# Householder steps of a tridiagonalization: fewer operations on GpSimd, a longer vector chain in another order

## The chip, the cores and the metric

One Trainium2 chip, one of its cores. The time is the device time in microseconds (us) of one execution of the whole program. A core has five engines with a queue each: PE (TensorE, matrix products), DVE (VectorE), ACT (ScalarE), POOL (GpSimd) and SP (SyncE, which issues the transfers here). Each engine works through its queue in order, and the engines meet only at semaphores.

## The reference, cut to what matters

A graph layer over a batch of 128 matrices `x[b]` of 120 nodes by 1024 features. One 120x120 adjacency matrix serves the whole batch:

```
degv = A.sum(0) + A.sum(1) - diagonal(A);  dinv = degv ** -0.5
Ln = dinv[:, None] * (diag(degv) - A) * dinv[None, :]
_, U = eigh(Ln)                                  # 120x120, once
h = relu(layernorm(x))                           # every b
agg = einsum('vn,bvd->bnd', U, h)
x1 = relu(agg @ W1 + b1) @ W2 + b2
... a non-local attention block over the 1024 positions (512 pooled keys) gives w_y ...
z = w_y + x1
out = x + einsum('nv,bvd->bnd', U, z) + z
```

The change is wholly inside `eigh`, in the reduction of `Ln` to tridiagonal form. That reduction is 118 Householder steps. With `v` the row of the remaining matrix below the pivot and `L = 120 - k` columns left in step `k`, a step makes the reflector `u = v + sign(v1)|v| e1`, scales it by `2/(u.u)`, and takes two rank-one products off the matrix, the second factor of which is `w = A u * scale + (a multiple) * u`.

## The kernel before, in words

The program has two phases. The first ends when the eigenvectors and everything folded into them are ready; until then it also does, for each batch element, the part of the layer norm and of the product with `W1` that doesn't need `U`. The second phase, 2685 us long, runs the attention block of every batch element and is not touched by the change.

In the first phase two chains run side by side:

- The eigenvectors, mostly on DVE. 118 Householder steps (`reflect`), then a grid count of eigenvalues, two finer sweeps, the vectors of the tridiagonal matrix, and their back-transformation. Of the latter, the product of all reflectors (`factor`) is made by PE, ACT and POOL beside DVE's work.
- The batch work ("pieces"), mostly on ACT. For batch element `t`, ACT makes relu and the sum of squares, PE transposes the result (4 pieces of 2 transposes, L684), ACT copies it out of PSUM (`fT`), PE multiplies it with `W1` (8 pieces of one product, L694), and ACT copies the result. That is 12 pieces for a batch element. ACT starts each with the relu of L533.

PE has one queue for both. Its order is written out by hand: in each Householder step it takes first the product for the row (L714), then some of the step's 9 pieces, then the two products of the rank-two update (L720, L721), then the rest of the pieces. The constant `LN_RATE` sets the 9, `LN_BEHIND` how many of them come after the update (2, so 7 come before it). After the last step the queue holds the remaining pieces, and among them `factor(i)` before batch element `WY_SLOT + 1 + i`, and the grid count's product (L791), which waits for DVE's grid, before batch element `GRID_AT` (98). Three small products that fold the vectors in (L772, L776, L780) stand after batch elements 127, 128 and 129.

One Householder step on DVE and its partners, by line:

- PE: L714 makes two rows, `A u`-like (partition 0 of `ps_V`) and the pivot row (partition 32).
- DVE: L1006 copies the pivot row to `row1`; L1008 adds `DU = sign * root` to `u[1]`; L1010 makes `z` from both rows and `DU`; L1012 makes `u.u`; L1014 the dot product of `u` and `z` (into `AC`); L1017 the reciprocal; L1020 times the gate (-1, or 0 for a null vector); L1022 `AC` times that; L1023 the scaled reflector `cu`; L1025 the second factor in place of `z`, which releases PE (`w_ready`).
- PE: L720, L721, the rank-two update into `ps_up`, which releases `up_ready`.
- DVE: L1029 and L1031 make the next `u` out of the row, `cu` and the second factor; L992 and L994 its squared norm without and with the first element (`XN`, `S2`); L1036 the next pivot column into `XI`; L1040 adds the update to `QA` in place, which releases the next step's L714 (`a_ready`); L1041 keeps a column.
- POOL (`shift`): L447 and L448 the sign, after `u_ready`; L450 the square root by `pow`, after `S2`; L451 `DU`, which L1008 waits for; L452 the gate. In steps 1 to 8 `fill` adds some memsets behind that.

In the code `need(i)` is a wait for DVE's own earlier instruction, `did` counts it, `T`, `TS` and `STT` are `tensor_tensor`, `tensor_scalar` and `scalar_tensor_tensor`.

## Time and profile before

| | |
|---|---|
| median of 3 runs | 3352.58 us (3351.86 to 3355.92) |
| the profiled execution: its own time | 3354.83 us |
| the profiled execution: span of the trace | 3353.1 us |
| granted TensorE clock, mean over the span | 0.989 of full |
| PE busy | 3181.8 us (95%) |
| DVE busy | 2289.5 us (68%) |
| ACT busy | 2413.1 us (72%) |
| POOL busy | 1949.6 us (58%) |

The span is the time from the first to the last instruction of one profiled execution; its own time is 1.7 us longer. PE's share is an average over two phases that are limited in different ways. A matmul row's duration includes a modelled end, so rows of PE overlap, and a busy PE isn't PE at its peak.

### The profile page before, as it was taken

To read this page: it belongs to the slowest core of one execution; us is meant where nothing else is said; L and a number is where in the kernel's file an instruction comes from. 1 tells how busy PE (TensorE), PEld (TensorE's weight loads), DVE (VectorE), ACT (ScalarE), POOL (GpSimd) and SP (SyncE) were. 2 spreads that over 40 slices of the span, in tenths; PEclk is the share of its full clock that TensorE was granted. 3 is DMA by queue.
4 is the path that set the end of the run, shared out by engine and by line. 5 is a ranking of instruction groups with operands and counts; after the bars stand their busy time and mean duration, and the time that the engine had idled before them with its cause. 6 is when DMAs were issued, how large, how long until landed. Compare 5 with 4: busy or idle time off the path is not lost.

```text
span 3353.1 us, 65817 instructions
## 1 busy us (share of the span) xinstructions
PE 3181.8 (95%) x16040; PEld 2554.4 (76%) x16040; DVE 2289.5 (68%) x6009; ACT 2413.1 (72%) x4380; POOL 1949.6 (58%) x2073
## 2 busy tenths in 40 slices
PE   6888886799999999999999999999999999999997
PEld 5667776677777777777777777778777777777775
DVE  7777778866666666666666666666666666666664
ACT  6888998856666766666666667666666676666665
POOL 4333321146666666666666666666666666666665
PEclk9999999989999999999999999999999999999998
DMA  3333433312222222222222222222222222222222
GB/s 95 93 96 98 105 107 95 95 37 72 74 75 75 73 71 71 71 71 72 73 74 72 71 71 71 71 71 71 73 74 74 75 71 71 71 71 71 73 74 67
DMA packets 111576, 256.22 MB, mean 76 GB/s; under 512 B 47501, under 2 KB 49798, under 8 KB 111494
## 3 DMA queue, kind: packets, MB, share of 16 engines
q1 hardware_dynamic: 111493, 255.25, 27.8%
q8 instruction: 37, 0.61, 0.1%
q14 instruction: 46, 0.37, 0.0%
HBM read 190.69 MB, written 63.44 MB: 76 GB/s over the span
## 4 chain that ended last, share of the span: by engine, by line
PE 80%; DVE 10%; POOL 3%; issue 3%; ACT 3%; DVEq 0%; POOLq 0%; ACTq 0%
PE ps_M L800 8%; PE ps_M L801 8%; PE ps_M L802 8%; PE ps_S L877 7%; PE ps_E L800 7%; PE ps_O L800 7%; PE ps_E L801 7%; PE ps_O L802 7%; PE ps_E L802 7%; PE ps_O L801 7%; PE ps_M L861 3%; POOL sc L450 1%; ACT junkx L537 1%; DVE u L1031 1%; DVE rown L1029 1%
## 5 line engine op out<-in xcount | busy, mean ns | idle before, releaser
L503 POOL TENSOR_TENSOR p_lo<-p,p_hi 128x512 fp32r<-128x512 f32 x1024 | 1380.9, 1349 | 932.1 <-ACT p_hi L654 929.9
L649 ACT ACTIVATE p<-ps_E 128x512 f32<-128x512 f32 x1024 | 613.6, 599 | 332.6 <-PE ps_E L802 307.5
L1394 DVE TENSOR_REDUCE nmx<-ps_S 128x1 f32<-128x512 f32 x1024 | 658.8, 685 | 127.8 <-PE ps_S L877 124.7
L654 ACT ACTIVATE p_hi<-p 128x512 fp32r<-128x512 f32 x1024 | 647.2, 632 | 32.6
L800 PE MATMUL ps_E<-o_hi,Q_hi 123*128 123x512 f32 x1024 | 427.0, 417 | 0.0
L800 PE MATMUL ps_O<-p_hi,v_hi 128*121 128x512 f32 x1024 | 407.2, 398 | 4.2 <-POOL p_lo L503 4.2
L802 PE MATMUL ps_O<-p_lo,v_hi 128*121 128x512 f32 x1024 | 406.7, 397 | 0.0
L801 PE MATMUL ps_E<-o_hi,Q_lo 123*128 123x512 f32 x1024 | 404.4, 395 | 0.0
L801 PE MATMUL ps_O<-p_hi,v_lo 128*121 128x512 f32 x1024 | 404.4, 395 | 0.0
L802 PE MATMUL ps_E<-o_lo,Q_hi 123*128 123x512 f32 x1024 | 404.2, 395 | 0.0
L1374 DVE TENSOR_REDUCE gf<-ps_M 128x256 f32<-128x512 f32 x256 | 177.1, 692 | 261.8 <-PE ps_M L802 261.8
L877 PE MATMUL ps_S<-Q_hi,o_hi 122*128 122x512 f32 x1024 | 349.7, 402 | 2.2 <-DVE nmx L1394 1.1
L510 POOL TENSOR_TENSOR y<-y,acc 121x512 f32<-121x512 f32 x256 | 329.0, 1285 | 13.3 <-DVE y L1402 13.3
L800 PE MATMUL ps_M<-o_hi,Chi 122*128 122x512 f32 (+1 forms) x768 | 314.0, 409 | 2.3 <-DVE o_lo L1359 1.5
L802 PE MATMUL ps_M<-o_lo,Chi 122*128 122x512 f32 (+1 forms) x768 | 303.1, 395 | 0.0
L801 PE MATMUL ps_M<-o_hi,Clo 122*128 122x512 f32 (+1 forms) x768 | 303.0, 394 | 0.0
L694 PE MATMUL ps_m<-W1s,fT 128*120 128x128 f32 x2048 | 285.0, 285 | 7.1 <-ACT P L549 7.1
L1365 DVE TENSOR_REDUCE phf<-ps_M 128x256 f32<-128x512 f32 x256 | 175.7, 686 | 130.0 <-PE ps_M L802 130.0
L694 PEld LDWEIGHTS ps_m<-W1s,fT 128*120 128x120 f32 x2048 | 245.3, 187 | 24.6 <-issue 16.1
L877 PEld LDWEIGHTS ps_S<-Q_hi,o_hi 122*128 122x128 f32 x1024 | 194.0, 190 | 80.0 <-ACT mrow L639 26.5
L621 ACT ACTIVATE o_hi<-ps_M 120x512 fp32r<-120x512 f32 x256 | 153.2, 598 | 139.1 <-PE ps_M L802 139.1
L800 PEld LDWEIGHTS ps_E<-o_hi,Q_hi 123*128 123x128 f32 x1024 | 193.8, 189 | 49.5 <-issue 6.4
(363 smaller groups left out, 5947.7 us busy)
## 6 DMA issues: line engine op xcount, KB each, us to landing
rbc<-r_dram SPq DMA_DIRECT2D x128, 484.0 KB
xin<-in_x_dram SPq DMA_DIRECT2D x128, 480.0 KB, 4.2
xt<-in_x_dram SPq DMA_DIRECT2D x128, 480.0 KB, 4.9
out_dram<-y SPq DMA_DIRECT2D x128, 480.0 KB, 3.7
o_hi<-mrow SPq DMA_DIRECT2D x256, 2.0 KB
dcol<-y SPq DMA_DIRECT2D x128, 4.0 KB, 2.0
r_dram<-rcol SPq DMA_DIRECT2D x128, 4.0 KB, 1.4
W1s<-in_L_gnn_W_dram SPq DMA_DIRECT2D x1, 512.0 KB, 4.1
```

The costliest lines, as they stand in the source:

```text
L503: pool.tensor_tensor(p_lo[:, c % 4, :], p[:, c % 4, :], p_hi[:, c % 4, :].bitcast(F32), ALU.subtract).then_inc(plo_sb, 1)
L510: pool.tensor_tensor(y[:, par, f], y[:, par, f], acc[:, par, f], ALU.add).then_inc(y_sb, 1)
L649: act.activation(p[:, c % 4, :], ps_E[c % 2][:, :], ACT.Exp).then_inc(p_sb, 1)
L654: act.activation(p_hi[:, c % 4, :], p[:, c % 4, :], ACT.Copy).then_inc(phi_sb, 1)
L694: last = mm(ps_m[par][0:N, 0:H], fT[:, par, c * N:(c + 1) * N], W1s[:, c, :], start=(c == 0), stop=(c == KC - 1))
L800: mm(dst, whi, mhi, start=start, stop=False)
L801: mm(dst, wlo, mhi, start=False, stop=False)
L802: return mm(dst, whi, mlo, start=False, stop=stop)
L877: mm(ps_S[SBANK[c]][:, :], o_hi[0:NA, par, c * 128:(c + 1) * 128], Q_hi[0:NA, par, :], start=True, stop=True).then_inc(S_ps, 1)
L1365: dve.tensor_reduce(phf[:, j * 256:(j + 1) * 256], ps_M[BANK["ph" + piece[2]]][:, :].rearrange("p (m t) -> p m t", t=2), AX.X, ALU.max).th ...
L1374: dve.tensor_reduce(gf[:, j * 256:(j + 1) * 256], ps_M[BANK["g" + piece[2]]][:, :].rearrange("p (m t) -> p m t", t=2), AX.X, ALU.max).then ...
L1394: dve.tensor_reduce(nmx[:, c:c + 1], ps_S[SBANK[c]][:, :], AX.X, ALU.max, negate=True).then_inc(max_sb, 1)
```

## The change

In words: GpSimd keeps the root of `S2` and gets one new operation, `TWICE = u1 * REC * GATE2`, which goes back to DVE. Sign and gates are made by DVE (`sign`), behind the `QA` update of the step before. The root goes straight into `u[1]`, before the row is there. The row is copied with the sign multiplied in, ahead of `u.u`. `RG` is gone: `cu` is `u` times the reciprocal times a gate that holds the factor 2. The first half of the next reflector (`rown`, the part with `cu[1]`) is made before the second factor, and reads its row from PSUM. Its second half uses `PAIR`, the second factor's first element, made from `TWICE`, `AC` and `z`'s first element instead of being read from the second factor. `QA` is held twice, each step reads one copy and writes the other, and the wait of the update for `XI` is gone. One copy at the end brings the even columns together. One piece more comes after the update in each step (`LN_BEHIND` 3), the grid product moves behind one more batch element (`GRID_AT` 99), and `factor` begins two batch elements earlier (`WY_SLOT` 94).

```
@@ gpsimd, shift(k)
-                pool.wait_ge(u_ready, k + 1)
-                chain(pool.tensor_scalar(sc[:, SGN:SGN + 1], u[:, 1:2], 0.0, 2.0, ALU.is_ge, ALU.mult))
-                chain(pool.tensor_scalar(sc[:, SGN:SGN + 1], sc[:, SGN:SGN + 1], -1.0, None, ALU.add))
                 pool.wait_ge(s2_ready, k + 1)
-                chain(pool.tensor_tensor(sc[:, ROOT:ROOT + 1], sc[:, S2:S2 + 1], sc[:, 11:12], ALU.pow))
-                pool.tensor_tensor(sc[:, DU:DU + 1], sc[:, SGN:SGN + 1], sc[:, ROOT:ROOT + 1], ALU.mult).then_inc(du_ready, 1)
-                pool.tensor_scalar(sc[:, GATE:GATE + 1], sc[:, XN:XN + 1], TINY, -1.0, ALU.is_gt, ALU.mult).then_inc(gate_ready, 1)
+                pool.tensor_tensor(sc[:, ROOT:ROOT + 1], sc[:, S2:S2 + 1], sc[:, 11:12], ALU.pow).then_inc(root_ready, 1)
+                if k + 1 < STEPS:
+                    pool.wait_ge(rec_ready, k + 1)
+                    pool.tensor_scalar(sc[:, TWICE:TWICE + 1], u[:, 1:2], sc[:, REC:REC + 1], sc[:, GATE2:GATE2 + 1],
+                                       ALU.mult, ALU.mult).then_inc(twice_ready, 1)
@@ tensor, reflect
-                mm(ps_V[0:33, 0:L], XI[:, k + 1:k + 34], QA[:, k:N], start=True, stop=True).then_inc(ry_ready, 1)
+                mm(ps_V[0:33, 0:L], XI[:, k + 1:k + 34], QA[:, par * N + k:par * N + N], start=True, stop=True).then_inc(ry_ready, 1)
@@ vector
+            def sign():
+                i_ge = did(TS(s_(SGN), u[:, 1:2], 0.0, 2.0, ALU.is_ge, ALU.mult))
+                did(TS(s_(GATE), s_(XN), TINY, -2.0, ALU.is_gt, ALU.mult))
+                did(TS(s_(GATE2), s_(XN), TINY, -4.0, ALU.is_gt, ALU.mult))
+                need(i_ge)
+                TS(s_(SGN), s_(SGN), -1.0, None, ALU.add).then_inc(sign_ready, 1)
...
             def reflect(k):
+                dve.wait_ge(root_ready, k + 1)
+                dve.wait_ge(sign_ready, k + 1)
+                i_u = did(STT(out=u[:, 1:2], in0=s_(ROOT), scalar=s_(SGN), in1=u[:, 1:2], op0=ALU.mult, op1=ALU.add))
                 dve.wait_ge(ry_ready, k + 1)
-                i_row = did(dve.tensor_copy(row1[:, k:N], ps_V[32:33, 0:L]))
-                dve.wait_ge(du_ready, k + 1)
-                i_u = did(T(u[:, 1:2], s_(DU), u[:, 1:2], ALU.add))
-                need(i_row)
-                i_z = did(STT(out=z_(0), in0=row1[:, k:N], scalar=s_(DU), in1=ps_V[0:1, 0:L], op0=ALU.mult, op1=ALU.add))
+                i_row = did(TS(row1[:, k:N], ps_V[32:33, 0:L], s_(SGN), None, ALU.mult))
                 need(i_u)
                 i_uu = did(STT(out=srow[:, k:k + 1], in0=u[:, 1:2], scalar=u[:, 1:2], in1=s_(XN), op0=ALU.mult, op1=ALU.add))
+                need(i_row)
+                i_z = did(STT(out=zt[:, 0:L], in0=row1[:, k:N], scalar=s_(ROOT), in1=ps_V[0:1, 0:L], op0=ALU.mult, op1=ALU.add))
+                need(i_uu)
+                dve.reciprocal(s_(REC), srow[:, k:k + 1]).then_inc(rec_ready, 1)
                 need(i_z)
-                i_dot = did(STT(out=sqj[:, 0:L], in0=u[:, 0:L], scalar=1.0, in1=z_(0), ..., accum_out=s_(AC)))
-                need(i_uu)
-                i_rec = did(dve.reciprocal(s_(REC), srow[:, k:k + 1]))
-                dve.wait_ge(gate_ready, k + 1)
-                need(i_rec)
-                i_rg = did(T(s_(RG), s_(REC), s_(GATE), ALU.mult))
-                need(i_rg)
-                i_ac = did(T(s_(AC), s_(AC), s_(RG), ALU.mult))
-                i_cu = did(TS(cu[:, 0:L], u[:, 0:L], s_(RG), 2.0, ALU.mult, ALU.mult))
-                need(i_ac)
-                STT(out=z_(0), in0=u[:, 0:L], scalar=s_(AC), in1=z_(0), op0=ALU.mult, op1=ALU.add).then_inc(w_ready, 1)
+                i_dot = did(STT(out=sqj[:, 0:L], in0=u[:, 0:L], scalar=0.5, in1=zt[:, 0:L], ..., accum_out=s_(AC)))
+                dve.wait_ge(rec_ready, k + 1)
+                i_cu = did(TS(cu[:, 0:L], u[:, 0:L], s_(REC), s_(GATE), ALU.mult, ALU.mult))
+                need(i_cu)
                 if k + 1 < STEPS:
-                    need(i_cu)
-                    dve.wait_ge(w_ready, k + 1)
-                    need(did(STT(out=rown[:, k + 2:N], in0=z_(2), scalar=cu[:, 1:2], in1=row1[:, k + 2:N], ...)))
-                    STT(out=u[:, 1:L - 1], in0=cu[:, 2:L], scalar=zs[:, N + 1:N + 2], in1=rown[:, k + 2:N], ...).then_inc(u_ready, 1)
+                    i_part = did(STT(out=rown[:, 0:L - 2], in0=zt[:, 2:L], scalar=cu[:, 1:2], in1=ps_V[32:33, 2:L], ...))
+                need(i_dot)
+                STT(out=zs[:, N:N + L], in0=cu[:, 0:L], scalar=s_(AC), in1=zt[:, 0:L], op0=ALU.mult, op1=ALU.add).then_inc(w_ready, 1)
+                now, then = par * N, (1 - par) * N
+                if k + 1 < STEPS:
+                    dve.wait_ge(twice_ready, k + 1)
+                    i_pair = did(STT(out=s_(PAIR), in0=s_(TWICE), scalar=s_(AC), in1=zt[:, 1:2], op0=ALU.mult, op1=ALU.add))
+                    need(i_part)
+                    need(i_pair)
+                    STT(out=u[:, 1:L - 1], in0=cu[:, 2:L], scalar=s_(PAIR), in1=rown[:, 0:L - 2], ...).then_inc(u_ready, 1)
                     dve.wait_ge(u_ready, k + 2)
+                    dve.wait_ge(w_ready, k + 1)
                     norm(L - 1)
                     dve.wait_ge(up_ready, k + 1)
                     STT(out=XI[:, k + 2:k + 3], ...).then_inc(xcol_ready, 1)
-                    dve.wait_ge(xcol_ready, k + 2)
                 dve.wait_ge(up_ready, k + 1)
-                T(QA[:, k:N], QA[:, k:N], ps_up[0:N, 1:L + 1], ALU.add).then_inc(a_ready, 1)
+                dve.wait_ge(a_ready, k + 1)
+                T(QA[:, then + k:then + N], QA[:, now + k:now + N], ps_up[0:N, 1:L + 1], ALU.add).then_inc(a_ready, 1)
+                if k + 1 < STEPS:
+                    sign()
                 dve.tensor_copy(wyCT[0:N, k:k + 1], ps_up[0:N, 0:1]).then_inc(c_kept, 1)
...
+            need(did(dve.tensor_copy(QA[:, 0:STEPS:2], QA[:, N:N + STEPS:2])))
@@ constants
-LN_RATE, LN_LEAD, LN_BEHIND = (9, 1), 2, 2
-GRID_AT = 98
-WY_SLOT, WY_STEPS = 96, 19
+LN_RATE, LN_LEAD, LN_BEHIND = (9, 1), 2, 3
+GRID_AT = 99
+WY_SLOT, WY_STEPS = 94, 19
```

## Rows read from the trace of the kernel before

**Rows 1.** Windows: stretch, its length, each engine's busy time (instructions), PEclk, DMA.

```profile
360.00:468.00 108.00, 94.27 (x729) 79.90 (x727) 79.46 (x574) 100.66 (x184) 41.65 (x150) 1.00 0.40 104
668.00:3353.00 2685.00, 2658.36 (x12159) 2114.35 (x12158) 1761.23 (x2816) 1843.60 (x3328) 1736.16 (x1406) 0.99 0.26 71
```

**Rows 2.** Timeline of one step (L=75): start, duration, engine, line, out<-in.

```profile
200.63 0.15 DVE L1008 TENSOR_TENSOR u<-sc,u 1x1 f32<-1x1 f32 x1
...
201.03 0.20 DVE L1012 SCALAR_TENSOR_TENSOR srow<-u,sc 1x1 f32<-1x1 f32 x1
201.16 0.22 DVE L1014 SCALAR_TENSOR_TENSOR sqj<-u,zs 1x75 f32<-1x75 f32 x1
...
201.31 0.15 DVE L1017 RECIPROCAL sc<-srow 1x1 f32<-1x1 f32 x1
...
201.56 0.15 DVE L1020 TENSOR_TENSOR sc<-sc 1x1 f32<-1x1 f32 x1
...
201.82 0.24 DVE L1023 TENSOR_SCALAR cs<-u,sc 1x75 f32<-1x75 f32 x1
...
201.99 0.28 DVE L1025 SCALAR_TENSOR_TENSOR zs<-u,sc,zs 1x75 f32<-1x75 f32 x1
...
202.37 0.28 DVE L1029 SCALAR_TENSOR_TENSOR rown<-zs,cs,row 1x73 f32<-1x73 f32 x1
...
202.69 0.28 DVE L1031 SCALAR_TENSOR_TENSOR u<-cs,zs,rown 1x73 f32<-1x73 f32 x1
```

**Rows 3.** Timeline, end of that step and start of the next.

```profile
202.59 0.37 PE L721 MATMUL ps_up<-cs,zs 1*120 1x76 f32 x2
...
203.27 0.21 DVE L994 SCALAR_TENSOR_TENSOR sc<-u,sc 1x1 f32<-1x1 f32 x1
203.39 0.21 POOL L448 TENSOR_SCALAR sc<-sc 1x1 f32<-1x1 f32 x1
203.41 0.20 DVE L1036 SCALAR_TENSOR_TENSOR XI<-ps_up,QA,strict 120x1 f32<-120x1 f32 x1
203.64 0.23 DVE L1040 TENSOR_TENSOR QA<-QA,ps_up 120x75 f32<-120x75 f32 x1
203.69 0.56 POOL L450 TENSOR_TENSOR sc<-sc 1x1 f32<-1x1 f32 x1
...
203.93 0.32 PE L714 MATMUL ps_V<-QA,XI 120*33 120x74 f32 x2 [0.41 <-DVE QA L1040]
...
204.33 0.18 POOL L451 TENSOR_TENSOR sc<-sc 1x1 f32<-1x1 f32 x1
...
204.54 0.15 DVE L1008 TENSOR_TENSOR u<-sc,u 1x1 f32<-1x1 f32 x1
```

**Rows 4.** All of L1040 (duration min/median/max, first and last start), one of them.

```profile
L1040 DVE TENSOR_TENSOR QA<-QA,ps_up x118: 158/219/279, 15.4 to 468.1; 120x120 f32<-120x120 f32 x1, 120x119 f32<-120x119 f32 x1, 120x118 f32<-120x118 f32 x1, 120x117 f32<-120x117 f32 x1
...
261.54 0.22 DVE L1040 TENSOR_TENSOR QA<-QA,ps_up 120x60 f32<-120x60 f32 x1
```

**Rows 5.** Timeline of ACT late in the first phase: two relus that follow each other.

```profile
640.46 1.17 ACT L533 ACTIVATE frelu<-xin,lns 120x1024 f32<-120x1024 f32 x1
...
644.75 1.17 ACT L533 ACTIVATE frelu<-xin,lns 120x1024 f32<-120x1024 f32 x1
```

**Rows 6.** Timeline: the grid product, and the end of the first phase.

```profile
526.97 0.56 PE L791 MATMUL ps_up<-ones,MJ 120*120 120x1 f32 x2 [11.52 <-DVE MJ L1172]
...
655.86 0.32 DVE L1316 TENSOR_SCALAR Z<-Z,pv 120x120 f32<-120x120 f32 x1
...
656.18 10.53 POOL L479 TENSOR_TENSOR rstd<-rstd,colA 120x64 f32<-120x64 f32 x1
656.27 0.29 DVE L1321 TENSOR_SCALAR wos<-wos,colA 120x128 f32<-120x128 f32 x1
...
659.42 0.27 PE L772 MATMUL ps_up<-ident,Z 120*120 120x120 f32 x1
...
666.79 0.76 POOL L498 TENSOR_TENSOR pst<-P,rstd 121x128 f32<-121x128 f32 x2
```

More of the change, by code:

```diff
@@ L102, in build @@
             row1 = eb("row1", [1, N])
+            zt = eb("zt", [1, N])
             rown = eb("rown", [1, N])
@@ L210, in build @@
         s2_ready = sem("s2_ready")
-        du_ready = sem("du_ready")
-        gate_ready = sem("gate_ready")
+        root_ready = sem("root_ready")
+        sign_ready = sem("sign_ready")
+        rec_ready = sem("rec_ready")
+        twice_ready = sem("twice_ready")
         w_ready = sem("w_ready")
@@ L1013, in reflect @@
+                need(i_uu)
+                dve.reciprocal(s_(REC), srow[:, k:k + 1]).then_inc(rec_ready, 1)
                 need(i_z)
-                i_dot = did(STT(out=sqj[:, 0:L], in0=u[:, 0:L], scalar=1.0, in1=z_(0), op0=ALU.mult, op1=ALU.mult,
+                i_dot = did(STT(out=sqj[:, 0:L], in0=u[:, 0:L], scalar=0.5, in1=zt[:, 0:L], op0=ALU.mult, op1=ALU.mult,
                                 accum_out=s_(AC)))
-                need(i_uu)
-                i_rec = did(dve.reciprocal(s_(REC), srow[:, k:k + 1]))
@@ L1018, in reflect @@
-                dve.wait_ge(gate_ready, k + 1)
-                need(i_rec)
-                i_rg = did(T(s_(RG), s_(REC), s_(GATE), ALU.mult))
-                need(i_rg)
-                i_ac = did(T(s_(AC), s_(AC), s_(RG), ALU.mult))
-                i_cu = did(TS(cu[:, 0:L], u[:, 0:L], s_(RG), 2.0, ALU.mult, ALU.mult))
-                need(i_ac)
-                STT(out=z_(0), in0=u[:, 0:L], scalar=s_(AC), in1=z_(0), op0=ALU.mult, op1=ALU.add).then_inc(w_ready, 1)
-                if k + 1 < STEPS:
-                    need(i_cu)
-                    dve.wait_ge(w_ready, k + 1)
-                    need(did(STT(out=rown[:, k + 2:N], in0=z_(2), scalar=cu[:, 1:2], in1=row1[:, k + 2:N],
-                                 op0=ALU.mult, op1=ALU.add)))
-                    STT(out=u[:, 1:L - 1], in0=cu[:, 2:L], scalar=zs[:, N + 1:N + 2], in1=rown[:, k + 2:N],
+                dve.wait_ge(rec_ready, k + 1)
@@ new lines, in reflect @@
+                i_cu = did(TS(cu[:, 0:L], u[:, 0:L], s_(REC), s_(GATE), ALU.mult, ALU.mult))
+                need(i_cu)
+                if k + 1 < STEPS:
+                    i_part = did(STT(out=rown[:, 0:L - 2], in0=zt[:, 2:L], scalar=cu[:, 1:2], in1=ps_V[32:33, 2:L],
+                                     op0=ALU.mult, op1=ALU.add))
+                need(i_dot)
+                STT(out=zs[:, N:N + L], in0=cu[:, 0:L], scalar=s_(AC), in1=zt[:, 0:L], op0=ALU.mult, op1=ALU.add).then_inc(w_ready, 1)
@@ L1032, in reflect @@
+                now, then = par * N, (1 - par) * N
[4 more added lines that the diff above has]
+                    need(i_pair)
+                    STT(out=u[:, 1:L - 1], in0=cu[:, 2:L], scalar=s_(PAIR), in1=rown[:, 0:L - 2],
                         op0=ALU.mult, op1=ALU.add).then_inc(u_ready, 1)
@@ L1033, in reflect @@
                     dve.wait_ge(u_ready, k + 2)
+                    dve.wait_ge(w_ready, k + 1)
                     norm(L - 1)
                     dve.wait_ge(up_ready, k + 1)
-                    STT(out=XI[:, k + 2:k + 3], in0=ps_up[0:N, 2:3], scalar=QA[:, k + 1:k + 2],
+                    STT(out=XI[:, k + 2:k + 3], in0=ps_up[0:N, 2:3], scalar=QA[:, now + k + 1:now + k + 2],
                         in1=strict[:, k + 1:k + 2], op0=ALU.add, op1=ALU.mult).then_inc(xcol_ready, 1)
-                    dve.wait_ge(xcol_ready, k + 2)
@@ L1410 @@
 PARAMS = 15
-XN, S2, ROOT, GATE, SGN, REC, DU, RG, AC = range(9)
+XN, S2, ROOT, GATE, GATE2, SGN, REC, PAIR, AC, TWICE = range(10)
 UNITS = 12
 TAIL_AT = B
-LN_RATE, LN_LEAD, LN_BEHIND = (9, 1), 2, 2
-GRID_AT = 98
-WY_SLOT, WY_STEPS = 96, 19
+LN_RATE, LN_LEAD, LN_BEHIND = (9, 1), 2, 3
+GRID_AT = 99
+WY_SLOT, WY_STEPS = 94, 19
 WY_T, WY_G = 1, 3
```

2 lines of the change are left out of this document (1 added, 1 removed).

## The prediction

> **What bounds the kernel now.** I read the windows first. In the second phase PE is busy for 2658 of 2685 us [rows 1], and nothing in that phase is changed, so the gain or loss lies in the first 668 us. Late in the Householder steps no engine is full (ACT 93%, PE 87%, DVE 74% of the stretch from 360 to 468 us) [rows 1]. The timeline of one step shows a closed circle of dependent instructions: from one L1008 at 200.63 to the next at 204.54, 3.91 us [rows 2, 3]. The starts of L1040 give the pace: 117 steps from 15.4 to 468.1 us, the first 60 of them until 261.54 at 4.10 us each, the other 57 at 3.62 [rows 4]. Last comes the join. DVE's eigenvectors are ready with L1316 at 655.86, and ACT's last square sum at about the same time, since POOL's L479 starts at 656.18 and the first matrix product of the second phase needs it, through L498 at 666.79 [rows 6]. Two chains that end together: both have to get shorter.
>
> Does ACT's chain follow? Where ACT alone sets the pace, a batch element takes 644.75 - 640.46 = 4.29 us [rows 5]. A step carries 9 of 12 pieces, so ACT needs 0.75 x 4.29 = 3.22 us a step. The steps now take more, so ACT is held back by them through PE's queue and follows them down to 3.22. After the steps the batch work stands at the same element as before, and later PE waits 11.5 us for the grid [rows 6], so ACT has slack there too. Hence a shorter step shortens both chains, down to about 3.22 us a step.
>
> **The circle, step by step (L=75).** Prices of a link first. An instruction that waits for DVE's previous one starts 0.04 us after its end. One that is independent of it starts 0.07 before its end (L1012 at 201.03 to L1014 at 201.16, with 0.20 of duration). Where two semaphores are waited for, the gap is 0.10 (L1017 to L1020, L1025 to L1029) [rows 2]. On POOL a chained instruction follows after 0.09 (L448 to L450), and DVE takes over 0.03 after POOL's end [rows 3].
>
> POOL first. The root L450 started 0.21 after the end of L994 (203.48), but 0.09 after the end of L448 (203.60): the sign held it up by about 0.13. With the sign gone it starts 0.08 after L994. L451 (0.18 and its gap of 0.08) also leaves the path. From the end of L994 to DVE's take-over were 204.54 - 203.48 = 1.06 us; now 0.08 + 0.56 + 0.10 = 0.74, with the double wait for root and sign. That is -0.32.
>
> DVE from there, counted from the start of the new `u` instruction (0.20, like L1012): row copy at 0.13, taken as 0.24 like L1023, until 0.37 (PE's row is there: below); `u.u` 0.30 to 0.50; `z` 0.43 to 0.71; reciprocal 0.64 to 0.79; dot product at 0.75, and 0.15 to the next, as L1014 to L1017; `cu` 0.90 to 1.14; first half of the next reflector 1.18 to 1.46; second factor 1.39 to 1.67; `PAIR` 1.60 to 1.80; second half at 1.84 if its two waits on one semaphore count as one, at 1.90 if not. I take 1.90. In the old step L1031 started at 202.69 - 200.63 = 2.06. The two removed one-element products (L1020 and L1022, 0.15 each with their gaps some 0.4) and the wait for the second factor pay for the longer head and for `PAIR`: -0.16. Behind it, L1031's start to L994's start took 0.58; the norm now waits for two semaphores, +0.06. Together 0.32 + 0.16 - 0.06 = 0.42: the circle falls from 3.91 to about 3.49 us.
>
> What could be late next. `TWICE`: the reciprocal ends at 0.79, `PAIR` can start at 1.60, and between them are a hand-over of 0.08, the instruction, and 0.03. A GpSimd instruction with two pointer scalars is in no row; 0.21 (L448) leaves 0.49 to spare, 0.56 (L450) still fits. The nearest is L448, so it costs nothing. `QA`: L994 starts at 2.54, `XI` 0.14 later as now, `QA` 0.13 later without its wait, until about 3.04; the row product then runs 3.10 to 3.42 (L714 starts 0.06 after L1040 ends), just ahead of 3.49 + 0.13. DVE's four sign instructions (0.15 each, 0.08 apart, one dependent) and the column copy end near 3.4, in the root's shade. Without that shade they would cost up to 0.45. The rank-two update: PE delivers L721 at 202.96, 0.69 after the end of L1025, so at 2.36, in time for `XI` at 2.68. PE's nine pieces: from 360 to 468 us it was busy 94.3 us in some 30 steps, 3.1 a step, and about 1.0 of that are the step's own three products, so a piece takes about 0.23; six fit before the update (from 0.0 to 1.67) and three between its end (2.36) and 3.10.
>
> A row that bears on the four sign instructions: POOL's L479, also a `pow` out of SBUF, runs for 10.53 us from 656.18, and DVE's TENSOR_SCALAR L1321 starts at 656.27 inside it and takes 0.29; L1316 before it took 0.32 for 120 elements beside another POOL instruction [rows 6]. Neither was kept waiting. The Trainium skill says otherwise, in "SBUF — State Buffer", section "Who interferes with whom": `tensor_scalar` in a two-port mode and a GpSimd instruction lock each other out of a shared port pair for the whole instruction, whoever is first. By that rule the sign instructions would stand behind the root until 3.4 and the circle would close near 3.9. The trace disagrees for this kind of instruction, so my sum goes by the row.
>
> **The sum.** The first 60 steps at -0.42 give 25 us. The other 57 would fall to 3.62 - 0.42 = 3.20 on average, and the later ones below ACT's 3.22; I take 3.27, since the two are coupled through PE's queue and some of each is lost: 57 x 0.35 = 20 us. Steps: -45 us. The final copy of the even columns adds about 0.3.
>
> The join: the grid product behind one element more lets ACT do 4.3 us of work in what was PE's wait of 11.5, so after the grid ACT's chain is 4.3 us shorter against DVE's. ACT then ends at 651.5 in the old clock, L479 at 662.4. DVE's Z stays at 655.9; L772 stood at 659.42 because of the pieces ahead of it [rows 6], and can come at about 656.4. From there to the second phase nothing changes: -3 us. `factor` two elements earlier only moves work into the same wait, 0.
>
> Total -48 us. For the profiled execution 3354.8 - 48 = 3307; the median shown is 2.3 us lower than that execution, so 3352.6 - 48 = 3304.6, say 3305 us.
>
> Bounds: a step's saving is 0.20 if the new double waits, the PSUM read of the half reflector and the row copy with a scalar each cost 0.07 more, 0.55 if none of the double waits shows. The late steps stand between 3.22 (ACT's rate) and 3.50 (no better than their end now). That spans 23 + 3 to 56 + 3 us of gain.
>
> **The rivals.**
>
> - The batch work holds the steps at about 3.50. For it: ACT is at 93% late in the steps, and PE has to serve both in one order. Against it: ACT's own need is 3.22, which leaves 0.28 between the two. Steps save 24 + 7.5 = 32, with the join 35: 3318 us. Chance 0.15.
> - Waits eat half the saving (0.27 a step, late steps at 3.25). For it: three new double waits. 31 + 3: 3319 us. Chance 0.12.
> - Sign stands behind root (the rule above as a mechanism of this step: circle at 3.85). For it: both read SBUF and overlap in time by design. Against it: the two rows cited. 7 + 3: 3343 us. Chance 0.05.
> - Slower. The round trip DVE to POOL to DVE for `TWICE` is new and in the middle of the circle; it decides from an instruction time of 0.70 us on, and eats the whole 0.42 at 1.12. POOL's durations go from 0.18 to 10.53 (that one on 64 columns), so an unlucky form at 1.5 us would make each step 0.38 slower: +44 us, 3397. For it: the form is in no row. Against it: one-element arithmetic without `pow` is at 0.18 to 0.22 in every POOL row of the step. Chance 0.03.
> - The join takes the gain, because ACT's chain as a whole can't end earlier. Against it: ACT needs 128 x 4.29 = 549 us in all, and with the 11.5 of the grid that is still well before 608. Chance 0.02, no change.
>
> **How the numbers follow.** The forecast has 0.63, with its own range of 3297 to 3312. Down to the bound of the highest saving it is 3293, and the two middling rivals lie at 3318 and 3319; the range 3292 to 3324 leaves out the rule's case and the slower one. A measurement of this kernel can tell about 0.2%, 7 us, from no change. Faster by more than that: 0.63 + 0.15 + 0.12 + 0.05 = 0.95; the same 0.02; slower 0.03.
>
> **What would show it.** L450 starts within 0.10 of L994's end. The new `u` instruction follows POOL's root by 0.03 to 0.10. The `TWICE` instruction is 0.2 to 0.3 long and done before `PAIR` is due. L1040's successor starts every 3.6 to 3.7 us in the first half and about 3.27 in the second; the last near 423. ACT is over 95% busy late in the steps. PE's idle before the grid product is 6 to 8 us instead of 11.5. The second phase starts near 620 and is as long as before. I am wrong if the circle closes over another path, above all the row product (L714) that waits behind three pieces of batch work, or if late steps wait for ACT's relu.

## The result and the profile after

The changed kernel takes 3326.88 us (median of 4 runs, 3326.38 to 3328.10) against 3353.23 us of the kernel before (4 runs, 3351.86 to 3355.92) beside it: a ratio of 0.9918 [0.9904, 0.9933]. That is 26.4 us less, where 48 were forecast.

First the windows of the changed kernel, for the late steps, the second phase, and the start of the latter. Columns: stretch, length, busy time (instructions) of PE, PEld, DVE, ACT and POOL, granted clock, DMA share, GB/s.

```profile
360.00:442.00 82.00, 76.59 (x611) 66.77 (x609) 73.26 (x558) 81.52 (x152) 22.07 (x50) 1.00 0.44 114
638.00:3325.00 2687.00, 2658.02 (x12160) 2113.05 (x12160) 1759.67 (x2818) 1843.74 (x3328) 1739.03 (x1408) 0.99 0.26 71
638.00:660.00 22.00, 15.65 (x37) 9.49 (x38) 10.14 (x19) 3.83 (x8) 0.76 (x2) 0.61 0.02 4
```

Late in the steps ACT is nearly full, 81.5 of 82 us, where it had 93% before [rows 1]. The second phase takes the 2687 us that it took before. So all of the gain lies ahead of 638 us, as forecast.

Next all instructions that add the update to `QA` (duration min/median/max, first and last start), then one step of the timeline, with 75 columns left in the next reflector: start, duration, engine, line, out<-in.

```profile
L1053 DVE TENSOR_TENSOR QA<-QA,ps_up x118: 148/208/271, 15.3 to 442.7; 120x120 f32<-120x120 f32 x1, 120x119 f32<-120x119 f32 x1, 120x118 f32<-120x118 f32 x1, 120x117 f32<-120x117 f32 x1
```

```profile
184.20 0.21 DVE L996 SCALAR_TENSOR_TENSOR sc<-u,sc 1x1 f32<-1x1 f32 x1
...
184.44 0.22 DVE L1049 SCALAR_TENSOR_TENSOR XI<-ps_up,QA,strict 120x1 f32<-120x1 f32 x1
184.49 0.54 POOL L450 TENSOR_TENSOR sc<-sc 1x1 f32<-1x1 f32 x1 [1.59 <-DVE sc L996]
...
184.72 0.14 DVE L1000 TENSOR_SCALAR sc<-u 1x1 f32<-1x1 f32 x1
...
184.85 0.32 PE L716 MATMUL ps_V<-QA,XI 120*33 120x77 f32 x2
184.90 0.13 DVE L1004 TENSOR_SCALAR sc<-sc 1x1 f32<-1x1 f32 x1
...
184.96 0.14 DVE L1056 COPY xt<-ps_up 120x1 f32<-120x1 f32 x1
...
185.14 0.21 DVE L1017 SCALAR_TENSOR_TENSOR u<-sc,u 1x1 f32<-1x1 f32 x1
185.38 0.29 DVE L1019 TENSOR_SCALAR row<-ps_V,sc 1x77 f32<-1x77 f32 x1
185.60 0.20 DVE L1021 SCALAR_TENSOR_TENSOR srow<-u,sc 1x1 f32<-1x1 f32 x1
185.83 0.28 DVE L1023 SCALAR_TENSOR_TENSOR zt<-row,sc,ps_V 1x77 f32<-1x77 f32 x1
...
186.29 0.38 POOL L453 TENSOR_SCALAR sc<-u,sc 1x1 f32<-1x1 f32 x1 [1.26 <-DVE sc L1025]
...
186.31 0.31 DVE L1030 TENSOR_SCALAR cs<-u,sc 1x77 f32<-1x77 f32 x1
186.65 0.28 DVE L1033 SCALAR_TENSOR_TENSOR rown<-zt,cs,ps_V 1x75 f32<-1x75 f32 x1
...
186.86 0.28 DVE L1036 SCALAR_TENSOR_TENSOR zs<-cs,sc,zt 1x77 f32<-1x77 f32 x1
...
187.07 0.20 DVE L1040 SCALAR_TENSOR_TENSOR sc<-sc,zt 1x1 f32<-1x1 f32 x1
...
187.38 0.28 DVE L1043 SCALAR_TENSOR_TENSOR u<-cs,sc,rown 1x75 f32<-1x75 f32 x1
...
187.96 0.21 DVE L996 SCALAR_TENSOR_TENSOR sc<-u,sc 1x1 f32<-1x1 f32 x1
```

The circle reads from the first L996 to the next: 187.96 - 184.20 = 3.76 us, against 3.91 before [rows 2, 3] and 3.49 in the forecast (medians of the steps 38 to 52: 3.75 against 3.90). Three late starts are to be seen. The row copy L1019 (185.38) needs nothing of L1017, and PE's product was done at 185.17, and yet it starts 0.03 after L1017's end (185.35). `z` (L1023, 185.83) needs the row, whose write ended at 185.67, and not `u.u`, but it starts 0.03 after the end of `u.u` (185.80). `XI` (L1049, 184.44) starts 0.03 after the end of L996, where before it started 0.07 ahead of it: L1036 at 203.41, L994 at 203.27 for 0.21 [rows 3].

The pace, from the `QA` starts of both traces [rows 4]: the first 60 steps fall from 4.10 to 3.93 us each, the other 57 from 3.62 to 3.36.

Last the timeline of the changed kernel at the grid and at the join. In brackets stand the idle time before an instruction and what ended it.

```profile
501.98 0.56 PE L793 MATMUL ps_up<-ones,MJ 120*120 120x1 f32 x2 [5.55 <-DVE MJ L1188]
...
626.04 10.53 POOL L481 TENSOR_TENSOR rstd<-rstd,colA 120x64 f32<-120x64 f32 x1
...
630.64 0.28 DVE L1332 TENSOR_SCALAR Z<-Z,pv 120x120 f32<-120x120 f32 x1
...
630.98 0.32 PE L774 MATMUL ps_up<-ident,Z 120*120 120x120 f32 x1 [1.54 <-DVE Z L1332]
...
638.31 0.76 POOL L500 TENSOR_TENSOR pst<-P,rstd 121x128 f32<-121x128 f32 x2 [1.74 <-DVE phf L1360]
```

PE waits 5.55 us for the grid instead of 11.52 [rows 6]. DVE's `Z` is ready at 630.92, and L774 follows it at once. `pst`, which opens the second phase, no longer waits for POOL's `pow` (over at 636.57) but for DVE. From the last `QA` to `pst` it is 638.31 - 442.71 = 195.6 us, before 666.79 - 468.11 = 198.7 [rows 4, 6]: the 3 us of the join are there.

The difference of the two spans, 3353.1 - 3325.2 = 27.9 us, adds up so: the first 60 steps 10.3, the other 57 15.1, the join 3.1, the second phase -0.6.

### The profile page after: what moved, and what is told of

It is laid out like the page before. It is cut to its first block, busy times and chain, and to the rows that moved or that the text cites. A ratio compares the mean times of both kernels' runs of the same rounds, so it can differ in the third digit from the quotient of the medians.

```text
span 3325.2 us, 65809 instructions
## 1 busy us (share of the span) xinstructions
PE 3168.9 (95%) x16040; PEld 2546.6 (77%) x16040; DVE 2322.8 (70%) x6363; ACT 2411.2 (73%) x4380; POOL 1890.5 (57%) x1718
## 4 chain that ended last, share of the span: by engine, by line
PE 80%; DVE 16%; issue 3%; POOL 1%; DMA 0%; ACT 0%; DVEq 0%; POOLq 0%; ACTq 0%
PE ps_M L802 8%; PE ps_M L803 8%; PE ps_M L804 8%; PE ps_S L879 7%; PE ps_E L802 7%; PE ps_O L802 7%; PE ps_E L803 7%; PE ps_O L804 7%; PE ps_E L804 7%; PE ps_O L803 7%; PE ps_M L863 3%; DVE ST L1133 1%; DVE row L1019 1%; DVE rown L1033 1%; DVE zt L1023 1%
```

## The experiments

Nine kernels, x8 cut from the kernel before and the others from the changed one, each timed beside the kernel before; the ratio is to it, on the same chip. Beside x1 to x4 the kernel before took 3353.8 us, beside x6 to x9 3352.8 and beside x10 3354.8, so a difference of 1 or 2 us between medians of different groups says nothing. x2, x7 and x10 leave a part of the computation out, as said at each; their times count, their results don't. Offsets are medians over steps 38 to 52, counted from the start of the `u` instruction (L1017), unless a row is shown.

| kernel | us | ratio to before | first 60 steps | other 57 | QA to pst |
|---|---|---|---|---|---|
| before | 3353.23 | 1 | 4.10 | 3.62 | 198.7 |
| changed | 3326.88 | 0.9918 [0.9904, 0.9933] | 3.93 | 3.36 | 195.6 |
| x1_same_partition | 3307.87 | 0.9859 [0.9844, 0.9874] | 3.78 | 3.20 | 195.6 |
| x2_no_pointer | 3313.73 | 0.9878 [0.9863, 0.9893] | 3.80 | 3.24 | 195.6 |
| x3_old_constants | 3326.05 | 0.9916 [0.9902, 0.9929] | 3.95 | 3.36 | 198.3 |
| x4_sign_early | 3322.22 | 0.9905 [0.9890, 0.9920] | 3.88 | 3.34 | 195.6 |
| x6_copy_before_sign | 3335.59 | 0.9949 [0.9932, 0.9965] | 4.01 | 3.43 | 195.3 |
| x7_half_from_copy | 3320.38 | 0.9906 [0.9889, 0.9922] | 3.85 | 3.34 | 195.4 |
| x8_root_only | 3351.27 | 0.9995 [0.9985, 1.0005] | 4.22 | 3.48 | 197.7 |
| x9_two_rates | 3303.50 | 0.9851 [0.9835, 0.9868] | 3.82 | 3.14 | 195.4 |
| x10_both | 3299.09 | 0.9831 [0.9814, 0.9847] | 3.72 | 3.17 | 195.5 |

### x1_same_partition: both rows in partition 0

```
-mm(ps_V[0:33, 0:L], XI[:, k + 1:k + 34], QA[...]).then_inc(ry_ready, 1)
+mm(ps_V[0:1, 256:256 + L], XI[:, k + 33:k + 34], QA[...])
+mm(ps_V[0:1, 0:L], XI[:, k + 1:k + 2], QA[...]).then_inc(ry_ready, 1)
-i_row  = ... ps_V[32:33, 0:L] ...         # row copy
+i_row  = ... ps_V[0:1, 256:256 + L] ...
-i_part = ... in1=ps_V[32:33, 2:L] ...     # half reflector
+i_part = ... in1=ps_V[0:1, 258:256 + L] ...
```

> The changed kernel (3326.9 us), with the pivot row made by a second product of one column on partition 0 of the same PSUM bank instead of partition 32. Theory A: a DVE instruction whose PSUM input starts at another partition than that of the last DVE instruction that read PSUM waits until all earlier DVE instructions have ended. Then at L=75 the row copy no longer starts 0.03 after the end of the new u instruction (0.24 after its start) but as soon as PE is done, z follows the row by 0.04 instead of u.u, and XI starts 0.14 instead of 0.24 after L996. A step at L=75 goes from 3.82 to about 3.6 us, the late ones not under 3.2: 3305 to 3312 us in all. Theory B: DVE holds every PSUM read in this order whatever the partition (or the width of the instructions explains the loss). Then the gaps stay 0.03 behind the previous end, and the second product on PE makes it the same or slower: 3327 to 3340 us.

19.0 us less than the changed kernel. The timeline of the same step (its lines lie one further on: 1018 is `u`, 1020 the row copy, 1022 `u.u`, 1024 `z`, 1050 `XI`):

```profile
178.77 0.21 DVE L997 SCALAR_TENSOR_TENSOR sc<-u,sc 1x1 f32<-1x1 f32 x1
...
178.91 0.20 DVE L1050 SCALAR_TENSOR_TENSOR XI<-ps_up,QA,strict 120x1 f32<-120x1 f32 x1
...
179.55 0.30 PE L717 MATMUL ps_V<-QA,XI 120*1 120x77 f32 x2
179.63 0.21 DVE L1018 SCALAR_TENSOR_TENSOR u<-sc,u 1x1 f32<-1x1 f32 x1
...
179.88 0.29 DVE L1020 TENSOR_SCALAR row<-ps_V,sc 1x77 f32<-1x77 f32 x1
180.10 0.20 DVE L1022 SCALAR_TENSOR_TENSOR srow<-u,sc 1x1 f32<-1x1 f32 x1
180.23 0.28 DVE L1024 SCALAR_TENSOR_TENSOR zt<-row,sc,ps_V 1x77 f32<-1x77 f32 x1
...
182.35 0.21 DVE L997 SCALAR_TENSOR_TENSOR sc<-u,sc 1x1 f32<-1x1 f32 x1
```

`z` starts 0.07 before the end of `u.u` (180.30), and `XI` 0.07 before the end of L997 (178.98). Neither does more or less work than in the changed kernel; only the partition in which PSUM is read, now or by the reader before, differs. The row copy still starts after `u` here, but the second product ends only at 179.85. Later in the steps the product is done sooner, and there the row copy's own start shows. With 50 columns in the row:

```profile
272.20 0.25 PE L717 MATMUL ps_V<-QA,XI 120*1 120x50 f32 x2
272.37 0.21 DVE L1018 SCALAR_TENSOR_TENSOR u<-sc,u 1x1 f32<-1x1 f32 x1
272.51 0.25 DVE L1020 TENSOR_SCALAR row<-ps_V,sc 1x50 f32<-1x50 f32 x1
```

The copy starts 0.07 before the end of `u` (272.58), where in the changed kernel it started 0.03 after it in these steps too, with the product done before. The circle takes 182.35 - 178.77 = 3.58 us with 77 columns. The theory that the starts are held by the partition stands; that they wait for the data or for the wider row product falls.

What ends the late steps here is ACT. Windows of this kernel:

```profile
360.00:424.00 64.00, 62.04 (x524) 53.18 (x523) 54.03 (x439) 64.00 (x120) 17.43 (x39) 1.00 0.43 116
```

ACT is busy for all of the 64 us, and the steps take 3.19 on average there: about the floor of 3.22 that the forecast had, now reached.

### x2_no_pointer: the one-element operands of two instructions taken out

```
-i_row = did(TS(row1[:, k:N], ps_V[32:33, 0:L], s_(SGN), None, ALU.mult))
+i_row = did(dve.tensor_copy(row1[:, k:N], ps_V[32:33, 0:L]))
-i_cu = did(TS(cu[:, 0:L], u[:, 0:L], s_(REC), s_(GATE), ALU.mult, ALU.mult))
+i_cu = did(TS(cu[:, 0:L], u[:, 0:L], s_(REC), -2.0, ALU.mult, ALU.mult))
```

> The changed kernel with the sign left out of the row copy (a plain copy) and the gate in cu replaced by the constant -2, so the reflector isn't the reference's. Theory C: each one-element operand read from memory lengthens a TENSOR_SCALAR by 0.06 to 0.07 us. Then at L=75 the row copy goes from 0.29 to 0.23 us and cu from 0.30 to 0.24, a step is 0.12 shorter where nothing else holds it: 3314 to 3320 us. Theory D: cu is long because GpSimd's TWICE runs beside it and reads the same elements. Then cu stays at 0.30: at most 3322 us.

13.2 us less than the changed kernel. The row copy in its timeline, with `z` to show that its hold is still there (0.03 after the end of `u.u`, 179.80):

```profile
179.44 0.23 DVE L1019 COPY row<-ps_V 1x77 f32<-1x77 f32 x1
179.60 0.20 DVE L1021 SCALAR_TENSOR_TENSOR srow<-u,sc 1x1 f32<-1x1 f32 x1
179.83 0.28 DVE L1023 SCALAR_TENSOR_TENSOR zt<-row,sc,ps_V 1x77 f32<-1x77 f32 x1
```

The row copy takes 0.23 instead of 0.29, and `cu` a median of 0.26 (0.24 to 0.28) instead of 0.31, over some 18 steps around this one. So each one-element operand that is read from memory, where there was a constant or none, costs about 0.05 or 0.06 on an instruction of 77 elements; 13.2 us over 118 steps is 0.11 for the two. Two reservations. The row's edit also changes the kind of instruction, from `TENSOR_SCALAR` to `COPY`, so the price of its operand isn't shown apart from that. And `cu` also depends on GpSimd's `TWICE` beside it. Within one step the lengths of the two change levels against each other: here, from step 43 to 44, `cu` gets 0.03 shorter and `TWICE` 0.05 longer, and in the changed kernel, from step 25 to 26, `cu` gets 0.04 shorter (0.35 to 0.31) and `TWICE` 0.07 longer (0.33 to 0.40). So theory D is not wholly out: 0.03 to 0.04 of `cu` in some of the steps is `TWICE` beside it, and x2 doesn't measure the operand apart from that.

### x3_old_constants: the order of the batch work as before the change

```
-LN_RATE, LN_LEAD, LN_BEHIND = (9, 1), 2, 3
-GRID_AT = 99
-WY_SLOT, WY_STEPS = 94, 19
+LN_RATE, LN_LEAD, LN_BEHIND = (9, 1), 2, 2
+GRID_AT = 98
+WY_SLOT, WY_STEPS = 96, 19
```

> The changed kernel with LN_BEHIND 2, GRID_AT 98 and WY_SLOT 96 as before. By the sum of the prediction the three constants bring 3 us at the join and nothing in the steps: 3330 us, with PE idle for some 11 us before the grid product and the steps as long as in the changed kernel. Rival: the third piece behind the update delays the next row product in the early steps; then undoing it makes the steps shorter and the kernel stays at 3327 us or falls.

The time is that of the changed kernel within the intervals, so this expectation missed. The trace has what was expected, and something else that hides it:

```profile
503.08 0.56 PE L793 MATMUL ps_up<-ones,MJ 120*120 120x1 f32 x2 [10.80 <-DVE MJ L1188]
...
631.54 10.53 POOL L481 TENSOR_TENSOR rstd<-rstd,colA 120x64 f32<-120x64 f32 x1
...
642.15 0.76 POOL L500 TENSOR_TENSOR pst<-P,rstd 121x128 f32<-121x128 f32 x2
```

The steps are no shorter (3.95 and 3.36 against 3.93 and 3.36), so the rival of this expectation, the third piece in the way of the row product, is out as well. PE waits 10.80 us for the grid, 5.25 more than in the changed kernel, ACT's chain is late by about as much, `pow` starts 5.5 us later than in the changed kernel and ends at 642.07, and `pst` follows it. From the last `QA` it takes 198.3 us, 2.7 more than in the changed kernel. But the second phase is 2.7 us shorter, 2684.2 against 2686.9. Its first 22 us, as a window of this kernel:

```profile
642.00:664.00 22.00, 15.80 (x46) 10.28 (x47) 11.96 (x20) 4.47 (x10) 0.83 (x3) 0.77 0.09 22
```

The granted clock is 0.77 of full there, against 0.61 in the changed kernel's window 638 to 660. Over all eleven traces the second phase, the same code in each, takes 2682.4 to 2689.3 us. The four with 0.77 at its start (x3, x4, x7, x8) lie at 2682.4 to 2685.2 and most others above, but x9, with 0.50, took 2684.7, so the clock at its start goes with the length without being shown as its cause. Either way, a join that is shorter in the trace by 3 us is not proven by the times, and small differences between the kernels are better read from the starts of `QA`.

### x4_sign_early: the sign made between the norm and XI

```
 i_xn = did(dve.tensor_tensor_reduce(... s_(XN)))
+i_ge = did(TS(s_(SGN), u[:, 1:2], 0.0, 2.0, ALU.is_ge, ALU.mult))
 need(i_xn)
 ...                                       # S2
+need(i_ge)
+TS(s_(SGN), s_(SGN), -1.0, None, ALU.add).then_inc(sign_ready, 1)
 # ... and u waits for root_ready alone; the wait for sign_ready stands behind QA
```

> The changed kernel with the sign made between the norm and XI instead of after QA. Theory E: the new u instruction is late because it waits for the sign, which ends after QA; then u starts 0.04 instead of 0.18 after the root's end at L=75 and XI 0.07 later, and the kernel gains some 4 us: 3323 us. Theory F: u starts 0.03 after the end of the column copy before it, because DVE can't take it earlier; then that distance stays, and the time is 3327 us or, with XI and QA later, up to 3332 us.

4.7 us less than the changed kernel, as expected (the intervals of the ratios overlap; in the trace the last `QA` starts 4.5 us earlier). By the trace, though, root and column copy end together here (182.91 and 182.92 in the step with 75 columns, `u` at 182.94), so it can't say whether the second wait or the row of instructions ahead of `u` was the cost. Hence the next one.

### x6_copy_before_sign: the sign ends last

```
 T(QA[...], ...).then_inc(a_ready, 1)
+dve.tensor_copy(wyCT[0:N, k:k + 1], ps_up[0:N, 0:1]).then_inc(c_kept, 1)
 if k + 1 < STEPS:
     sign()
-dve.tensor_copy(wyCT[0:N, k:k + 1], ps_up[0:N, 0:1]).then_inc(c_kept, 1)
```

> The changed kernel with the column copy ahead of the four sign instructions instead of behind them. Theory E (the new u instruction waits for the sign, whose own semaphore takes 0.10 us): the sign ends 0.07 later, so u does too, QA to u goes from 0.56 to 0.62 us at L=75: 3327 to 3333 us. Theory F (u starts 0.03 to 0.04 after the end of whatever DVE did last before it): the last one is now the sign, which ends at the same place as the copy did, u stays at QA + 0.56 and the time at 3327 us.

8.7 us more than the changed kernel, with the same instructions in another order: the direction of theory E, though 2.6 us above the range that it gave. From `QA` to the next `u` it is 0.62 instead of 0.56, as expected, some 7.5 us over 118 steps. Its timeline:

```profile
188.11 0.54 POOL L450 TENSOR_TENSOR sc<-sc 1x1 f32<-1x1 f32 x1 [1.59 <-DVE sc L996]
...
188.34 0.15 DVE L1054 COPY xt<-ps_up 120x1 f32<-120x1 f32 x1
...
188.59 0.13 DVE L1004 TENSOR_SCALAR sc<-sc 1x1 f32<-1x1 f32 x1
...
188.82 0.21 DVE L1017 SCALAR_TENSOR_TENSOR u<-sc,u 1x1 f32<-1x1 f32 x1
```

The root ends at 188.65, the last sign instruction at 188.72, and `u` starts 0.10 after the latter. In the changed kernel the last sign instruction ends at 185.03 and `u` starts 0.11 after it, although the copy, the last of DVE's instructions there, ends at 185.10. DVE's instructions together end 0.90 after the start of `S2` in both (188.72 - 187.82, 185.10 - 184.20), so their number does not explain the difference; the end of the sign does. The trace shows where the 0.10 comes from: of the two waits in front of `u`, the one written last (for the sign) is an instruction by itself, `EVENT_SEMAPHORE` at L1016, 0.02 long, once in each of the 118 steps. It starts 0.04 after the sign's end, and `u` 0.07 after its start. Where the sign is older, `u` follows the root by 0.04 with both waits kept (x1, x7), and by 0.03 with the sign's wait moved away (x4). The 0.10 doesn't hang on who made the value: in x8 the row copy has two waits, PE's product in the last, and starts 0.11 after that product's end, against 0.04 with one wait in the kernel before. That writing the wait for the later value first would save the 0.07 was not tried.

### x7_half_from_copy: the half reflector reads the copied row

```
-    i_ge = did(TS(s_(SGN), u[:, 1:2], 0.0, 2.0, ALU.is_ge, ALU.mult))
+    i_ge = did(TS(s_(SGN), u[:, 1:2], 0.0, 0.0, ALU.is_ge, ALU.mult))
 ...
-    TS(s_(SGN), s_(SGN), -1.0, None, ALU.add).then_inc(sign_ready, 1)
+    TS(s_(SGN), s_(SGN), 1.0, None, ALU.add).then_inc(sign_ready, 1)
 ...
-    i_part = did(STT(..., scalar=cu[:, 1:2], in1=ps_V[32:33, 2:L], ...))
+    i_part = did(STT(..., scalar=cu[:, 1:2], in1=row1[:, k + 2:N], ...))
```

The copied row has the sign in it, so the sign is fixed at +1, by the same number of instructions, and the result is not the reference's.

> The changed kernel with the sign fixed at +1 (the same four instructions) and the first half of the next reflector reading the row from its copy in SBUF, so that L1033 no longer reads PSUM at partition 32 before XI reads it at partition 0. Theory A (an instruction whose PSUM input starts at another partition than the last PSUM input waits for all before it): XI starts 0.14 instead of 0.24 after L996, QA and the sign come 0.10 earlier, u 0.07 earlier (then the root binds), the row copy and z still start as before: 3319 to 3324 us. Theory B (order alone): XI stays at 0.24 and the time at 3327 us.

6.5 us less than the changed kernel by the medians, 4 by the ratios; in the trace the last `QA` starts 5.9 us earlier (436.86 against 442.71). `XI` in its timeline, behind the instruction for `S2`, and the head of the next step:

```profile
180.68 0.21 DVE L996 SCALAR_TENSOR_TENSOR sc<-u,sc 1x1 f32<-1x1 f32 x1
...
180.82 0.20 DVE L1049 SCALAR_TENSOR_TENSOR XI<-ps_up,QA,strict 120x1 f32<-120x1 f32 x1
...
182.01 0.20 DVE L1021 SCALAR_TENSOR_TENSOR srow<-u,sc 1x1 f32<-1x1 f32 x1
182.24 0.28 DVE L1023 SCALAR_TENSOR_TENSOR zt<-row,sc,ps_V 1x77 f32<-1x77 f32 x1
```

`XI` has its early start again (0.14 after the start of `S2`), while `z` keeps its late one, 0.03 after the end of `u.u` (182.21); in the medians row and `z` stand at 0.24 and 0.69 as before the edit. With x1 this ties each held start to the reader of PSUM before it: the half reflector reads partition 32, `XI` partition 0; the column copy partition 0, the row partition 32; then `z` partition 0.

### x8_root_only: the kernel before, with the short GpSimd chain

```
 # gpsimd, shift(k): sign, DU and gate gone
+pool.tensor_tensor(ROOT, S2, ..., ALU.pow).then_inc(du_ready, 1)
 # vector: sign() behind the QA update (gate with -1.0), DU by DVE; all else as before
+i_du = did(T(s_(DU), s_(ROOT), s_(SGN), ALU.mult))
+i_u = did(STT(out=u[:, 1:2], in0=s_(ROOT), scalar=s_(SGN), in1=u[:, 1:2], ...))
```

> The kernel before (3353.8 us here) with one part of the change alone: GpSimd keeps only the root, sign and gate are made by DVE behind QA, and DU by one DVE instruction behind the row copy. Theory G: until about L=60 the old step was held by two paths that ended together, GpSimd's DU and the row product with its copy, so shortening GpSimd's alone brings nothing there and the added instruction costs about 0.05 a step; only late steps, where DVE stood 0.3 waiting for DU, gain some 0.15: 3345 to 3355 us. The prediction's reading, where the hand-over to GpSimd was the one path that shrinks, would give up to 0.25 a step: 3325 us.

No change in the time. GpSimd answers sooner, but in the middle steps the circle stays at 3.93 us (before 3.90), since the row copy waits for PE's product (its lines: 1010 the row copy, 1012 `DU`, 1013 `u`, 1015 `z`):

```profile
198.12 0.54 POOL L447 TENSOR_TENSOR sc<-sc 1x1 f32<-1x1 f32 x1 [3.42 <-DVE sc L989]
...
198.93 0.23 DVE L1010 COPY row<-ps_V 1x77 f32<-1x77 f32 x1 [0.19 <-PE ps_V L709]
...
199.16 0.20 DVE L1013 SCALAR_TENSOR_TENSOR u<-sc,u 1x1 f32<-1x1 f32 x1
199.39 0.28 DVE L1015 SCALAR_TENSOR_TENSOR zs<-row,sc,ps_V 1x77 f32<-1x77 f32 x1
```

The root is ready at 198.66, and `DU` comes at 199.09, behind the row copy. In the kernel before, GpSimd's `DU` and the row copy ended within 0.02 of each other (medians). Late in the steps, where `QA` is short and the row earlier, the gain shows: 3.32 us instead of 3.53 (medians of steps 100 to 114).

The first 60 steps are slower by 0.11 each, and the traces say why: the experiment also lengthens the row's path. `DU` now stands behind the row copy, and `u` takes 0.20 instead of 0.15. From the start of the row copy to that of `z` it is 0.48 us in steps 15 to 29 (before 0.37), 0.46 in steps 38 to 52 (before 0.44) and 0.39 in steps 100 to 113 (before 0.60). The double wait only moved: the row copy starts 0.07 later behind the product, and the gap of 0.07 at the gate is gone. What the late steps win, the early ones lose. So x8 shows that until about the middle of the steps the short GpSimd chain brings nothing while `DU` stands behind the row copy. What it would bring in the middle steps without that added instruction is not shown.

### x9_two_rates: x1 with another pace of the batch work

```
-wanted = max(0, (k - LN_LEAD) * LN_RATE[0] // LN_RATE[1])
+wanted = max(0, (min(k, 60) - LN_LEAD) * 10) + max(0, k - 60) * 8
```

> The kernel with both rows on partition 0 (3307.9 us), with 10 pieces of batch work in each step up to the 60th and 8 in each later one instead of 9. Theory H: its late steps (3.20 us on average) are held by ACT's 0.75 x 4.29 = 3.22 us a step and not by DVE's circle, and early ones have ACT idle. With 8 pieces ACT needs 2.86, so the last 57 steps fall to some 3.05 on average and the first 60 stay: 3298 to 3303 us. Rival: DVE's circle sets the late steps too; then nothing changes, 3308 us, or the tenth piece delays the early row products and it is slower.

It has x1's edits too. The time is just above the 3298 to 3303 us that were expected. Eight pieces a step instead of nine lower ACT's floor, and the steps 100 to 114 go from 3.13 to 2.99 us; the first 60, with ten, pay 0.04. The other 57 came to 3.14 on average, where 3.05 was expected. This is the fastest version here that computes everything, 23.4 us less than the changed kernel, but its interval and x1's overlap, so the two are not told apart by the times.

### x10_both: x1 and x2 together

The edits are those of x1 and x2; like x2 it leaves out the sign in the row and the gate.

> Both edits together: the two rows on partition 0 (3307.9 us alone) and no one-element operands in the row copy and in cu (3313.7 us alone; the sign is left out of the row and the gate is the constant -2). If the held starts and the one-element operands are the whole of what the prediction missed, the circle at L=75 closes near the 3.49 us that it forecast (3.42: 3.54 less 0.12), the first 60 steps take 3.66 us on average, the late ones stay at ACT's 3.2, and the kernel comes to 3298 to 3304 us. If something else is missing, or the two overlap, it stays near 3308 us.

3299.09 us (3297.70 to 3302.25), in the expected range. With both costs gone the circle closes in 3.43 us (median), where this expectation had 3.42 and the forecast 3.49; the first 60 steps take 3.72, where 3.66 was expected. The two are enough to explain the miss. Item by item it is not the forecast's circle: the row copy still starts at 0.23, since it waits for the product, the instruction that makes the next `u` starts at 1.96 against 1.90, and the rest of the circle is 0.12 shorter than in the sum (the norm's second wait costs nothing, and the root binds and not the sign).

The gains of x1 and x2 one by one, 19.0 + 13.2 = 32.2, are more than the 27.8 together. By the starts of `QA` they add up in full from the 10th to the 90th step (16.9 + 9.7 against 26.7). They are lost at both ends: in the first ten steps x10 is 3.4 us slower than the changed kernel, with the row copy of steps 7 and 8 1.67 us after `u` and waiting for PE's product, and from the 90th on it gains nothing, with ACT busy for all of the last 59 us of the steps.

## Why the prediction missed

The direction was right, and so was the kind of gain, a shorter circle. The size was not: 26.4 us of 48, and the time is 3 us outside the range.

**The step that failed is "DVE from there".** It let each instruction that is independent of its predecessor start 0.07 before its end, from one pair of rows (L1012, L1014) [rows 2] that read SBUF alone. The row was set at 0.13 and came at 0.24; `z` at 0.43 and came at 0.69, with reciprocal, dot product and all behind it. In medians `z` is 0.26 late: 0.11 for the start of the row, 0.05 for its length, 0.10 for its own start. With 0.06 for the length of `cu` the next `u` instruction (L1043) came at 2.23 against 1.90. That a change of partition causes the late start of `z` is shown by x1, where it stands at 0.56, and that of the row by x1's later steps, where it starts 0.14 after `u` once the product is early.

The kernel before held its readers in the same way. Its row copy was made while DVE waited for `DU`, so that hold cost nothing. But its `z` was held on the circle, and a row of the trace before showed it:

```profile
200.38 0.23 DVE L1006 COPY row<-ps_V 1x75 f32<-1x75 f32 x1 [0.34 <-PE ps_V L714]
...
200.82 0.28 DVE L1010 SCALAR_TENSOR_TENSOR zs<-row,sc,ps_V 1x75 f32<-1x75 f32 x1
```

This `z` (partition 0, after the row copy at partition 32) needs the row, whose write ended at 200.61, and `DU`, and nothing of L1008. Yet it starts 0.04 after the end of L1008 (200.78) and not 0.07 before it. The forecast took its price for an independent instruction from the pair that reads SBUF and passed over this one. The change then put three such starts into the step: the row, `z` and `XI`. The Trainium skill has the rule, in "VectorE: DVE Perf Modes", section "Two Vector instructions with no wait between them": an instruction with a PSUM input that starts in another group of 32 partitions than the first PSUM input of the last instruction that read PSUM starts only when all earlier ones have finished. The trace agrees at row, `z` and `XI`, and x1 and x7 show it.

The forecast's own sum with row and `z` late by 0.11 and 0.10 gives, as an estimate from these offsets, a circle of 3.70; x2, which has these holds without the operands from memory, closes in 3.63.

**The price of the row copy with a scalar** was taken as 0.24 and is 0.29 (in the bounds it had 0.07 more, in the sum nothing); `cu` went from 0.24 to 0.30 with its gate from memory. By x2 the two are 13 us of the 22 that the forecast missed.

**The double waits.** At the norm I took 0.06, and it cost nothing (L1043 to the next L996 0.58, as L1031 to L994 before). At root and sign 0.10 was taken, and the step has it, though by the sign (x6), not by the root. From the end of `S2` to `u` it took 0.73 against the forecast 0.74: GpSimd's part was right. But until about the middle of the steps the row's path ended with GpSimd's, so a shorter GpSimd chain needs the moved row copy to be worth its 0.32, and x8, which has the first without the second, gained nothing there. The forecast counted the two together, without saying that one needs the other.

**XI** was taken 0.14 after `S2` and came at 0.24. It pushes `QA` and the sign back by as much, until the sign ends with the root (185.03) and its 0.10 decides over the root's 0.03. In the forecast's sum this was no loss, since the 0.10 was in it, but it is one that could be had back: x7 puts it at some 6 us.

**By stretch.** The circle at L=75 saved 0.16 instead of 0.42, and the first 60 steps 10.3 us instead of 25. The other 57 saved 15.1 of 20: from 3.53 to 3.21 in the steps 100 to 114, where GpSimd's shorter chain shows by itself (x8), and less ahead of them. ACT's floor was right (x1, x9). In the changed kernel it hardly binds: two relus follow each other in 4.37 us on average from 360 to 442, against 4.31 in x1.

**The range.** The forecast's lowest saving of 0.20 a step, with the join, is 26 us by its own sum, a time of 3327, and with its late steps at 3.50 it is 22 us; yet its range ended at 3324, where the middling rivals stand. The measured time is at that lower bound. The saving of the first 60 steps, 0.17 each, is below it. The rival of 3319 is also added up wrong: 0.27 a step and late steps at 3.25 make 16 + 21 + 3 = 40 us, 3312.

**Right:** L450 0.08 after the end of `S2`; PE's wait for the grid (forecast 6 to 8, 5.55 measured); the join's 3 us in the trace; the second phase as long as before. `TWICE` is longer than I said, 0.38, but ends at 186.67, 0.40 ahead of `PAIR` (187.07): hidden. Of the rivals, the one that let the sign stand behind the root is refuted: L1000 to L1004 run at 0.13 each inside the root's 184.49 to 185.03. "Waits eat half the saving" gave 3319 and comes nearest in kind, but it named the waits for semaphores, and those were not the cause.

Open: what x8's short GpSimd chain is worth without its added instruction, what sets the level of the clock at the start of the second phase, and what makes that phase 2682 to 2689 us long.
